# Moving the reciprocal row sums of a two-layer attention kernel by DMA through DRAM, instead of by widening, TensorE transposes and a ScalarE copy

## The chip, the cores and the metric

The kernel runs on one core of one Trainium2 chip. The metric is the device time in microseconds (us) of one execution. Some operations are named by engine: PE is TensorE, DVE is VectorE, ACT is ScalarE, POOL is GpSimd, SP is the engine whose queue issues the DMAs.

## The reference

Eight sequences of 256 tokens and width 256 pass through a gated routing layer (L0) and then through a transformer block. The block is self-attention (16 heads of 64), cross-attention to a context of 120 tokens, and a gated feed-forward layer of inner width 1024, each with a layer norm before it and a residual after it. The part that the change touches is the softmax of both attentions:

```python
h = layernorm(x, ln1_g, ln1_b)
x = attention(h, h, a1_Wq, a1_Wk, a1_Wv, a1_Wo, a1_bo) + x
h = layernorm(x, ln2_g, ln2_b)
x = attention(h, context, a2_Wq, a2_Wk, a2_Wv, a2_Wo, a2_bo) + x
# attention: attn = softmax(q k^T * SCALE); out = (attn @ v) @ Wo + bo
```

All of it is float32. Products are made from two rounded parts of each operand (hi and lo, three matmuls for one product).

## The kernel before

After L0 (to about 215 us) come 128 attention steps, `STEPS = 2 * B * PAIRS`: for each of the two attentions, for each sequence b of 8, for each pair of heads i of 8. Step G has b = G // 8 (0 to 7 self, 8 to 15 cross) and i = G % 8. Then come 8 feed-forward blocks (from about 935 us). Each engine has its own instruction list, written out by hand in `step_self(G)`, `step_cross(G)` and `feed_forward(b)`, and the engines meet only at semaphores. So the order on each engine is fixed, and an instruction that waits holds up all that stands behind it.

What happens to one pair of heads G:

- PE `scores(G)`, one step ahead; DVE `row_max(G)`; ACT `softmax_pair(G)` writes the unnormalised p and its row sums `expsum`, tokens on the partitions.
- DVE `inverse_sums(G)` (line 1096) opens DVE's step G: the reciprocal `rsum`, 128 tokens x (2 token tiles x 2 heads).
- PE `transpose_p(G)` (L1523), ACT `round_pT` (L731) and DVE `pT_low` (L1103) bring p into transposed hi and lo parts.
- PE `weighted_values(G)` in step G + 1 makes the output o in the transposed layout, 64 dimensions of each head on the partitions and 256 tokens in the free direction, in columns 0 to 255 of PSUM bank 6.
- Row sums stand per token, and in o the tokens lie along the free direction. So POOL `widen_sums(G)` (L531) copies each reciprocal 64 times into `rsw`, PE transposes `rsw` with two 128x128 transposes into columns 256 to 511 of bank 6 (L1538, the first thing that `weighted_values` does), and ACT `copy_rT(G)` (L735) brings that into SBUF as `rT`. The result is the reciprocal, repeated over the 64 partitions of each head.
- DVE `normalise_o(G)` (L1111), the last thing in DVE's step G + 1, multiplies o by `rT`; POOL `split_o(G)` splits the product; PE `project_out` uses it.

`weighted_values(G)` waits for `normalise_o(G - 1)`, because both use bank 6. Once per sequence comes the hand-over: `residual`, layer norm (`prepare_*`), storing and loading of the tokens by SP. Where two phases meet (b = 0, 7, 8 and 15), ACT and DVE also split the next weights (`weights_hi` L290, `weights_lo` L300), which SP loads in units of two 256 KB DMAs into four slots (`load_weights`, waits on `w_ready`). SP's list before is one loop over the 24 sequence turns: load, store, now and then a context or weights.

Of the kernel before, what the change touches and what calls it, by code (L numbers as in the profile page):

```python
# [26 lines left out]
NT = S // 128  # L27
# [93 lines left out]
def build(nc, x, ctx_p, weights, params, rows, ident_in, x1_dram, x2_dram, x3_dram, out):  # L121
    es = ExitStack()
    with es:
        def sb(name, shape, dt=F32, where=es):
            return where.enter_context(nc.sbuf_tensor(name, shape, dt))
# [78 lines left out]
        with ExitStack() as l1:  # L204
# [7 lines left out]
            with ExitStack() as att:  # L212
# [10 lines left out]
                rsw = sb("rsum_wide", [128, 2, NT, 2 * DH], where=att)  # L223
                rT = sb("rsumT", [128, S], where=att)
# [37 lines left out]
            "rsum_wide", "pT", "pT_hi", "pT_lo", "o", "rT_copied", "o_norm", "o_hi", "o_lo", "wo", "up", "gelu", "glu",  # L262
            "f_hi", "f_lo", "down")}
        NI = B // L0B

# [101 lines left out]
        def _(sp):  # L367
# [63 lines left out]

            load(0)
            load_context(B)
            load(1)
            load(2)
            for b in range(3 * B):
                if b + 3 < 3 * B:
                    load(b + 3)
                store(b)
                if B < b + 3 < 2 * B:  # L440
                    load_context(b + 3)
                if b == 0:
                    load_weights(sp, 12, 16)
                if b == 6:
                    load_weights(sp, 16, 20)
                if b == 8:
                    load_weights(sp, 20, 24)
                if b == 14:
                    load_weights(sp, 24, 26)
# [4 lines left out]
        def _(pool):  # L454
# [74 lines left out]
            def widen_sums(G):  # L529
                pool.wait_ge(y["rsum"], G + 1)  # L530
                nc.gpsimd.tensor_tensor(rsw[:, G % 2, :, :].rearrange("p t (e d) -> p (t e) d", e=2),  # L531
                                        rs[:, G % 2, :].unsqueeze(2).broadcast_to([128, NT * 2, DH]),
                                        ones[:, :].rearrange("p (n d) -> p n d", d=DH), ALU.mult
                                        ).then_inc(y["rsum_wide"], 1)

# [7 lines left out]
            def step(G):  # L543
                b, i = divmod(G, PAIRS)
                widen_sums(G)
# [20 lines left out]
        def _(act):  # L566
# [166 lines left out]
            def copy_rT(G):  # L733
                act.wait_ge(y["o"], G + 1)
                nc.scalar.copy(rT[:, :], bank[6][:, S:2 * S]).then_inc(y["rT_copied"], 1)  # L735

# [18 lines left out]
            def step_self(G):  # L755
# [31 lines left out]
                if G >= 1:  # L787
                    copy_rT(G - 1)

            def step_cross(G):  # L790
# [26 lines left out]
                copy_rT(G - 1)  # L817

            def feed_forward(b):
                it = b - 2 * B  # L820
                for j in range(FF // 128):
# [7 lines left out]
                    if j == 1 and it == 0:  # L829
                        copy_rT(STEPS - 1)  # L830
                        weights_hi(act, 25)
# [972 lines left out]
```

## Time and profile before

| | us |
|---|---|
| median of 3 runs (lowest, highest) | 1088.32 (1087.79, 1089.55) |
| profiled execution, its own time | 1088.15 |
| its span, first to last instruction | 1086.4 |
| PE busy in the span | 997.5 (92%) |
| DVE busy | 710.9 (65%) |
| ACT busy | 626.5 (58%) |
| POOL busy | 357.2 (33%) |
| mean granted TensorE clock | 0.969 of full speed |

The matmuls are pipelined: the duration of one is longer than the distance to the next, so a busy PE is not a measure of its rate. The distance from start to start is. What an operation is worth is read from the stretch in which it stands and from what ends last there.

### The profile page before, as it was taken

The numbers are of one execution on the slowest core, as the hardware profiler recorded it, in microseconds if no ns is written. First come the engines' busy times: TensorE is split into PE (matmuls) and PEld (weight loads), VectorE is DVE, ScalarE is ACT, GpSimd is POOL, SyncE is SP. The second block draws the span as 40 slices with busy tenths as digits, with TensorE's granted clock in tenths as the row PEclk, the third lists the DMA queues.
The fourth block names the chain that finished last, engine by engine and source line by source line (L and its number), as shares of the span: only waits on it lengthen the run. The fifth ranks groups of instructions, "written<-read, shape, count | busy, mean of one in ns | idle before, by whom it ended". The sixth has DMA issues, their size and how long they took to land.

```text
span 1086.4 us, 21327 instructions
## 1 busy us (share of the span) xinstructions
PE 997.5 (92%) x7872; PEld 937.3 (86%) x7872; DVE 710.9 (65%) x1598; ACT 626.5 (58%) x1945; POOL 357.2 (33%) x474
## 2 busy tenths in 40 slices
PE   5688874599999999999999999999999998899998
PEld 4577753489999999899999899999999997899998
DVE  4466744596766676667667775666677667566664
ACT  3466452386656575657566765666666666533333
POOL 1101324033334333333333244454554454401010
PEclk9999887699999999999999998999999999999999
DMA  6221000100200000000000300300000001010100
GB/s 205 68 68 39 20 20 20 44 11 2 98 2 21 1 21 1 21 1 21 2 21 3 101 25 1 103 25 2 25 26 18 8 21 46 17 38 21 40 30 21
DMA packets 28121, 34.62 MB, mean 32 GB/s; under 512 B 2164, under 2 KB 21364, under 8 KB 28020
## 3 DMA queue, kind: packets, MB, share of 16 engines
q1 hardware_dynamic: 28020, 33.26, 9.9%
q8 instruction: 65, 1.06, 0.4%
q14 instruction: 36, 0.29, 0.1%
HBM read 24.86 MB, written 8.39 MB: 31 GB/s over the span
## 4 chain that ended last, share of the span: by engine, by line
PE 79%; DVE 10%; ACT 6%; issue 2%; POOL 1%; DMA 1%; SPq 1%; DVEq 0%; POOLq 0%
PE bank L1306 17%; PE bank L1307 16%; PE bank L1308 16%; PE bank L1523 8%; PE bank L1506 5%; PE bank L1564 3%; PE bank L1565 3%; PE bank L1566 3%; PE bank L1538 3%; ACT p L721 1%; PE bank L1480 1%; PE bank L1414 1%; DVE bn L887 1%; PE bank L1415 1%; PE bank L1416 1%
## 5 line engine op out<-in xcount | busy, mean ns | idle before, releaser
L721 ACT ACTIVATE p<-bank,negmax 128x256 f32<-128x256 f32 (+1 forms) x512 | 208.2, 428 | 18.0 <-DVE negmax L1088 15.1
L538 POOL TENSOR_TENSOR oT_hi<-oT,ones 128x256 fp32r<-128x256 f32 x128 | 94.0, 735 | 378.0 <-DVE oT L1111 378.0
L731 ACT CAST pT_hi<-bank 128x512 fp32r<-128x512 f32 (+1 forms) x256 | 110.7, 485 | 166.1 <-PE bank L1523 165.3
L1306 PE MATMUL bank<-hT_hi,w_hi 128*128 128x256 f32 x640 | 190.6, 298 | 5.9 <-DVE hT_lo L1072 2.5
L1308 PE MATMUL bank<-hT_hi,w_lo 128*128 128x256 f32 x640 | 181.5, 284 | 0.0
L1307 PE MATMUL bank<-hT_lo,w_hi 128*128 128x256 f32 x640 | 181.3, 283 | 0.0
L1306 PEld LDWEIGHTS bank<-hT_hi,w_hi 128*128 128x128 f32 x640 | 122.6, 192 | 9.2 <-DVE hT_lo L1072 4.8
L1103 DVE TENSOR_TENSOR pT_lo<-bank,pT_hi 128x512 fp32r<-128x512 f32 (+1 forms) x256 | 129.7, 548 | 0.3
L1084 DVE TENSOR_REDUCE negmax<-bank 128x2 f32<-128x512 f32 x128 | 82.2, 684 | 66.8 <-PE bank L1506 66.8
L1307 PEld LDWEIGHTS bank<-hT_lo,w_hi 128*128 128x128 f32 x640 | 122.9, 192 | 0.0
L1308 PEld LDWEIGHTS bank<-hT_hi,w_lo 128*128 128x128 f32 x640 | 122.6, 192 | 0.0
L1306 PE MATMUL bank<-pT_hi,v_hi 128*128 128x256 f32 (+1 forms) x384 | 119.5, 311 | 0.0
L721 ACT ACTIVATION_READ_ACCUMULATOR p<-bank,negmax 128x1 f32 x512 | 110.2, 215 | 0.0
L1307 PE MATMUL bank<-pT_lo,v_hi 128*128 128x256 f32 (+1 forms) x384 | 109.1, 284 | 0.0
L1523 PE MATMUL bank<-ident,p 128*128 128x128 f32 (+1 forms) x768 | 109.1, 278 | 0.1
L1308 PE MATMUL bank<-pT_hi,v_lo 128*128 128x256 f32 (+1 forms) x384 | 109.0, 284 | 0.0
L540 POOL TENSOR_TENSOR oT_lo<-oT,oT_hi 128x256 fp32r<-128x256 f32 x128 | 95.1, 743 | 10.0
L1523 PEld LDWEIGHTS bank<-ident,p 128*128 128x128 f32 (+1 forms) x768 | 83.6, 140 | 9.0 <-ACT p L721 0.5
L531 POOL TENSOR_TENSOR rsum_wide<-rsum,ones 128x256 f32<-128x256 f32 x128 | 80.1, 626 | 17.6 <-DVE rsum L1096 17.6
L825 ACT ACTIVATE p<-bank,params_pp 128x256 f32<-128x256 f32 x64 | 30.4, 475 | 82.5 <-PE bank L1308 82.4
L1307 PEld LDWEIGHTS bank<-pT_lo,v_hi 128*128 128x128 f32 (+1 forms) x384 | 74.1, 193 | 0.0
L1308 PEld LDWEIGHTS bank<-pT_hi,v_lo 128*128 128x128 f32 (+1 forms) x384 | 74.0, 193 | 0.0
(200 smaller groups left out, 2787.2 us busy)
## 6 DMA issues: line engine op xcount, KB each, us to landing
w_stage<-in_weights SPq DMA_DIRECT2D x52, 256.0 KB, 4.8
x_in<-x_dram SPq DMA_DIRECT2D x24, 256.0 KB, 2.9
x_dram<-x_out SPq DMA_DIRECT2D x16, 256.0 KB, 3.2
l_x<-in_x SPq DMA_DIRECT2D x4, 512.0 KB, 5.6
x_dram<-l_out SPq DMA_DIRECT2D x4, 512.0 KB, 2.9
out_dram<-x_out SPq DMA_DIRECT2D x8, 256.0 KB, 3.1
l_ctx<-in_ctx SPq DMA_DIRECT2D x4, 240.0 KB, 5.3
ctx_in<-in_ctx SPq DMA_DIRECT2D x8, 120.0 KB, 3.2
```

Source lines behind the costliest of these rows:

```text
L531: nc.gpsimd.tensor_tensor(rsw[:, G % 2, :, :].rearrange("p t (e d) -> p (t e) d", e=2), rs[:, G % 2, :].unsqueeze(2).broadcast_to([128, NT ...
L538: nc.gpsimd.tensor_tensor(oh[:, G % PAIRS, :], of[:, :], ones[:, :], ALU.mult).then_inc(y["o_hi"], 1)
L540: nc.gpsimd.tensor_tensor(ol[:, G % PAIRS, :], of[:, :], oh[:, G % PAIRS, :].bitcast(F32), ALU.subtract).then_inc(y["o_lo"], 1)
L721: last = nc.scalar.activation(p[:, G % 2, e, t * cols:(t + 1) * cols], scores_at(G, e, t), ACT.Exp, bias=negmax[:, G % 2, t, e:e + 1], acc ...
L731: nc.scalar.copy(pTh[0:r, G % 2, e, 0:n], bank[4 + e][0:r, 0:n]).then_inc(y["pT_hi"], 1)
L1084: nc.vector.tensor_reduce(negmax[:, G % 2, :, e], score_bank(G, e)[:, :].rearrange("p (t n) -> p t n", t=NT), AX.X, ALU.max, negate=True). ...
L1103: nc.vector.tensor_tensor(pTl[0:r, G % 2, e, 0:n], bank[4 + e][0:r, 0:n], pTh[0:r, G % 2, e, 0:n].bitcast(F32), ALU.subtract).then_inc(y[" ...
L1306: nc.tensor.matmul(dst, lh, rh, start=(i == 0), stop=False)
L1307: nc.tensor.matmul(dst, lh, rl, start=False, stop=False)
L1308: last = nc.tensor.matmul(dst, ll, rh, start=False, stop=(i == n - 1))
L1506: last = nc.tensor.matmul(score_bank(G, e)[:, t * S:(t + 1) * S], lhs[pr, g, 0, tt], rhs[pr, g, 1, :], start=(n == 0), stop=(n == 2))
L1523: last = nc.tensor.transpose(bank[4 + e][0:n, j * S + t * 128:j * S + (t + 1) * 128], p[:, G % 2, e, t * cols + j * 128:t * cols + j * 128 ...
```

## The change

- `widen_sums`, the two transposes of `weighted_values` and `copy_rT` are gone, with the buffer `rsw` and the wait of PE for it.
- `inverse_sums` writes `rsum` ordered head, token tile, and waits that the DMA of two steps before has read the buffer.
- SP gets `spread_sums(G)`: it waits for `rsum`, writes 2 KB to DRAM (256 runs of two numbers, 8 bytes each, since the row in DRAM is ordered token, token tile), waits until that has landed, and issues two DMAs that read a row of 1 KB and write it to 64 partitions each. `rT` is now double.
- `normalise_o` waits for both DMAs and for PE's o, and reads `rT` with a stride of two numbers.
- SP's list is written anew around `spread_sums`: one call for each step, with stores at i = 3, loads at i = 4, contexts at i = 5, and the units of weights one by one, each behind a `spread_sums`.

```diff
-                rsw = sb("rsum_wide", [128, 2, NT, 2 * DH], where=att)
-                rT = sb("rsumT", [128, S], where=att)
+                rT = sb("rsumT", [128, 2, S], where=att)
...
+        sums_dram = nc.dram_tensor("rsums_dram", (2, 2, S), F32, kind="Internal").ap()
...
+            def spread_sums(G):
+                sp.wait_ge(y["rsum"], G + 1)
+                if G >= 2:
+                    sp.wait_ge(y["rT"], 32 * (G - 1))
+                sp.dma_start(sums_dram[G % 2, :, :].rearrange("e (q t) -> q e t", t=NT),
+                             rs[:, G % 2, :].rearrange("q (e t) -> q e t", e=2)).then_inc(y["rsum_row"], 16)
+                sp.wait_ge(y["rsum_row"], 16 * (G + 1))
+                if G >= 2:
+                    sp.wait_ge(y["o_norm"], G - 1)
+                for e in range(2):
+                    sp.dma_start(rT[e * DH:(e + 1) * DH, G % 2, :], sums_dram[G % 2, e:e + 1, :].partition_broadcast(DH)
+                                 ).then_inc(y["rT"], 16)
...
-            load(2)
-            for b in range(3 * B):
-                if b + 3 < 3 * B:
-                    load(b + 3)
-                store(b)
-                if B < b + 3 < 2 * B:
-                    load_context(b + 3)
-                if b == 0:
-                    load_weights(sp, 12, 16)
-                if b == 6:
-                    load_weights(sp, 16, 20)
-                if b == 8:
-                    load_weights(sp, 20, 24)
-                if b == 14:
-                    load_weights(sp, 24, 26)
+            for G in range(STEPS):
+                b, i = divmod(G, PAIRS)
+                spread_sums(G)
+                if i == 3 and b >= 1:
+                    store(b - 1)
+                if i == 4:
+                    load(b + 2)
+                if i == 5 and B < b + 2 < 2 * B:
+                    load_context(b + 2)
+                if b == 1 and i < 4:
+                    load_weights(sp, 12 + i, 13 + i)
+                if b == B - 1 and i >= 2 and i < 6:
+                    load_weights(sp, 14 + i, 15 + i)
+                if b == B + 1 and i < 4:
+                    load_weights(sp, 20 + i, 21 + i)
+                if b == 2 * B - 1 and i in (6, 7):
+                    load_weights(sp, 18 + i, 19 + i)
+            store(2 * B - 1)
+            for b in range(2 * B, 3 * B):
+                if b + 2 < 3 * B:
+                    load(b + 2)
+                store(b)
...
             def inverse_sums(G):
                 dve.wait_ge(y["exp"], 2 * G + 2)
-                nc.vector.reciprocal(rs[:, G % 2, :], expsum[:, G % 2, :, :].rearrange("p t e -> p (t e)")
+                if G >= 2:
+                    dve.wait_ge(y["rsum_row"], 16 * (G - 1))
+                nc.vector.reciprocal(rs[:, G % 2, :].rearrange("p (e t) -> p e t", e=2), expsum[:, G % 2, :, :].rearrange("p t e -> p e t")
...
             def normalise_o(G):
-                dve.wait_ge(y["rT_copied"], G + 1)
+                dve.wait_ge(y["rT"], 32 * (G + 1))
+                dve.wait_ge(y["o"], G + 1)
...
-                nc.vector.tensor_tensor(of[:, :], bank[6][:, 0:S], rT[:, :], ALU.mult).then_inc(y["o_norm"], 1)
+                nc.vector.tensor_tensor(of[:, :].rearrange("p (t q) -> p t q", t=NT),
+                                        bank[6][:, 0:S].rearrange("p (t q) -> p t q", t=NT),
+                                        rT[:, G % 2, :].rearrange("p (q t) -> p t q", t=NT), ALU.mult).then_inc(y["o_norm"], 1)
...
-                pe.wait_ge(y["rsum_wide"], G + 1)
...
-                for t in range(NT):
-                    nc.tensor.transpose(bank[6][:, S + t * 128:S + (t + 1) * 128], rsw[:, G % 2, t, :], ident[:, :])
```

## Rows read from the trace of the kernel before

**Rows 1.** The page: busy time of the engines, and the lines of the chain.

```profile
PE 997.5 (92%) x7872; PEld 937.3 (86%) x7872; DVE 710.9 (65%) x1598; ACT 626.5 (58%) x1945; POOL 357.2 (33%) x474
PE bank L1306 17%; PE bank L1307 16%; PE bank L1308 16%; PE bank L1523 8%; PE bank L1506 5%; PE bank L1564 3%; PE bank L1565 3%; PE bank L1566 3%; PE bank L1538 3%; ACT p L721 1%; PE bank L1480 1%; PE bank L1414 1%; DVE bn L887 1%; PE bank L1415 1%; PE bank L1416 1%
```

**Rows 2.** Windows, self stage and cross stage: length, busy (count), clock, DMA.

```profile
215.00:580.00 365.00, 364.27 (x3128) 337.11 (x3127) 254.09 (x528) 236.85 (x722) 128.71 (x184) 1.00 0.05 17
...
660.00:905.00 245.00, 239.69 (x1994) 233.82 (x1994) 165.56 (x416) 160.51 (x647) 118.85 (x169) 1.00 0.08 25
```

**Rows 3.** Waits of PE, 220 to 940 us: total, times, longest.

```profile
PE bank L1538 <- DVE oT L1111: 14.3, 11, 2.3
```

**Rows 4.** Timeline of PE in a self step: start, duration, instruction.

```profile
405.86 0.28 PE L1308 MATMUL bank<-hT_hi,w_lo 128*128 128x256 f32 x1
405.99 0.38 PE L1538 MATMUL bank<-ident,rsum_wide 128*128 128x128 f32 x2
...
406.32 0.28 PE L1307 MATMUL bank<-pT_lo,v_hi 128*128 128x256 f32 x1
406.44 0.28 PE L1308 MATMUL bank<-pT_hi,v_lo 128*128 128x256 f32 x1
```

**Rows 5.** Timeline of PE, the same place in a cross step.

```profile
776.19 0.28 PE L1308 MATMUL bank<-hT_hi,w_lo 128*128 128x256 f32 x1
...
776.65 0.28 PE L1307 MATMUL bank<-pT_lo,v_hi 120*128 120x256 f32 x1
```

**Rows 6.** Groups of PE by form, and of ACT: busy, mean ns, idle before.

```profile
L1538 PE MATMUL bank<-ident,rsum_wide 128*128 128x128 f32 x256 | 49.5, 275 | 14.3 <-DVE oT L1111 14.3
...
L735 ACT COPY rsumT<-bank 128x256 f32<-128x256 f32 x128 | 49.4, 386 | 8.7 <-PE bank L1308 1.1
```

**Rows 7.** Timeline of DVE in a self sequence, reciprocal and normalisation of G = 30.

```profile
402.28 0.17 DVE L1096 RECIPROCAL rsum<-expsum 128x4 f32<-128x4 f32 x1
...
414.75 0.41 DVE L1111 TENSOR_TENSOR oT<-bank,rsumT 128x256 f32<-128x256 f32 x1
```

**Rows 8.** Timeline of DVE in a cross sequence, G = 91, and one sequence later.

```profile
760.10 0.17 DVE L1096 RECIPROCAL rsum<-expsum 128x4 f32<-128x4 f32 x1
...
767.56 0.42 DVE L1111 TENSOR_TENSOR oT<-bank,rsumT 128x256 f32<-128x256 f32 x1 [0.84 <-ACT rsumT L735]
...
797.85 0.17 DVE L1096 RECIPROCAL rsum<-expsum 128x4 f32<-128x4 f32 x1
```

**Rows 9.** Timeline of PE: the transposes that follow the normalisation of G = 91.

```profile
771.45 0.38 PE L1538 MATMUL bank<-ident,rsum_wide 128*128 128x128 f32 x2
```

**Rows 10.** DMA issues, KB, us to landing: page; 1060 to 1090 us; timeline of SP.

```profile
x_in<-x_dram SPq DMA_DIRECT2D x24, 256.0 KB, 2.9
x_dram<-x_out SPq DMA_DIRECT2D x16, 256.0 KB, 3.2
...
out_dram<-x_out SPq DMA_DIRECT2D x2, 256.0 KB, 2.1
...
l_rows_bc<-in_rows SPq DMA_DIRECT2D x3, 128.0 KB, 4.4
...
3.76 1.38 SPq L397 DMA_DIRECT2D l_rows_bc<-in_rows  x3
```

**Rows 11.** Timelines of DVE and PE in the last cross sequence.

```profile
920.49 1.22 DVE L300 TENSOR_TENSOR w_lo<-w_stage,w_hi 128x1024 fp32r<-128x1024 f32 x1 [1.89 <-ACT w_hi L290]
921.63 0.42 DVE L1111 TENSOR_TENSOR oT<-bank,rsumT 128x256 f32<-128x256 f32 x1
...
922.19 0.41 PE L1538 MATMUL bank<-ident,rsum_wide 128*128 128x128 f32 x2 [2.25 <-DVE oT L1111]
```

**Rows 12.** Timelines where the last weights are split: DVE, then PE.

```profile
926.70 0.17 DVE L1096 RECIPROCAL rsum<-expsum 128x4 f32<-128x4 f32 x1
...
937.64 0.38 PE L1538 MATMUL bank<-ident,rsum_wide 128*128 128x128 f32 x2
```

**Rows 13.** Window after a wait in the first cross sequence; the clock is third from last.

```profile
648.00:656.00 8.00, 8.00 (x41) 8.00 (x39) 2.75 (x7) 3.60 (x13) 3.31 (x5) 0.50 0.01 3
```

More of the change, by code:

```diff
@@ L261, in build @@
             "cT_hi", "cT_lo", "qk", "qk_hi", "qk_lo", "v", "v_hi", "v_lo", "scores", "negmax", "exp", "rsum",
-            "rsum_wide", "pT", "pT_hi", "pT_lo", "o", "rT_copied", "o_norm", "o_hi", "o_lo", "wo", "up", "gelu", "glu",
+            "rsum_row", "rT", "pT", "pT_hi", "pT_lo", "o", "o_norm", "o_hi", "o_lo", "wo", "up", "gelu", "glu",
             "f_hi", "f_lo", "down")}
         NI = B // L0B
+        sums_dram = nc.dram_tensor("rsums_dram", (2, 2, S), F32, kind="Internal").ap()
         def wcols(name, kt, lo_col, n):
@@ L527, in add_bias @@
                                         ALU.add).then_inc(y["xb"], 1)
[L529 to L534, printed above, removed]
             def split_o(G):
@@ L544, in step @@
                 b, i = divmod(G, PAIRS)
-                widen_sums(G)
                 if i == 0:
@@ L731, in round_pT @@
                     nc.scalar.copy(pTh[0:r, G % 2, e, 0:n], bank[4 + e][0:r, 0:n]).then_inc(y["pT_hi"], 1)
-            def copy_rT(G):
-                act.wait_ge(y["o"], G + 1)
-                nc.scalar.copy(rT[:, :], bank[6][:, S:2 * S]).then_inc(y["rT_copied"], 1)
             def round_self(b, g):
@@ L786, in step_self @@
                     weights_hi(act, 10 + i)
-                if G >= 1:
-                    copy_rT(G - 1)
             def step_cross(G):
@@ L816, in step_cross @@
                     weights_hi(act, 17 + i)
-                copy_rT(G - 1)
             def feed_forward(b):
@@ L829, in feed_forward @@
                     if j == 1 and it == 0:
-                        copy_rT(STEPS - 1)
                         weights_hi(act, 25)
```

## Prediction

> **What bounds the kernel now.** I read the busy times first: PE is busy for 92% of the span, the next engine, DVE, for 65% [rows 1]. Matmuls overlap here, so that alone proves little. The chain of what ended last says the same by another way: its long shares are all PE lines, and the transposes at L1538, which the change removes, hold 3% of it [rows 1]. The windows by stage then show where. In 365 us of the self stage PE is idle for 0.7 us; in 245 us of the cross stage for 5.3 us; the granted clock is 1.00, the 2.4 GHz level, in both [rows 2]. The waits of PE name one cause almost alone: the first instruction of `weighted_values` waits 11 times, 14.3 us in all, for `normalise_o` of DVE [rows 3]. So in nearly every one of the 128 steps PE is what ends last. Work taken off PE comes off the time, while work taken off ACT and POOL does not by itself.
>
> **What goes.** Two transposes in each step. Their group is busy for 49.5 us, 275 ns each [rows 6], but what counts is the distance they put between neighbours. From the last projection matmul to the second matmul of `weighted_values` it is 406.32 - 405.86 = 0.46 us; undisturbed neighbours stand 0.12 us apart, so two such distances would be 0.24, and the pair costs 0.22 us [rows 4]. The cross stage has 776.65 - 776.19 = 0.46 at the same place, so 0.22 again [rows 5]. Times 64 that is 14.1 us in each stage, 28.2 in all.
>
> The Trainium skill ("TensorE: Matmul & The Clock Gate", Part 4) gives about 275 ns for such a transpose in a kernel, and says that the 2.4 GHz level does not engage for transposes. The first agrees with the duration here, but as a cost for 256 of them it would make 70 us, and start to start the trace gives less than half. The second the trace contradicts: the clock is 1.00 through the self stage with these transposes in every step.
>
> From that 28.2 I take what PE can't use:
>
> - *Self.* PE has next to no wait to hide in. Where the phases meet, ACT and DVE are loaded with weights; I let two steps go, 0.4 us. Left: 13.7.
> - *Cross.* Once in each sequence PE waits for `normalise_o`, and the pair that stands just before is parallel to DVE's chain (scale and shift, the hi part, `hT_lo`, `v_lo`, `normalise_o`). That pair only lengthens the wait: 8 pairs. In the last cross sequence DVE waits for ACT's high part of the weights, makes the low part (1.22), then `normalise_o`, and PE waits 2.25 us behind that [rows 11]. This ring has no transpose of the sums and no copy in it, so 4 more pairs are lost. 12 x 0.22 = 2.6. At the 11 waits themselves the transposes stand behind the wait; part of what they cost is the change of PE from float32 transposes to split matmuls, which the transposes of p cause as well. I take 0.05 less for each, 0.6. Left: 14.1 - 2.6 - 0.6 = 10.9.
>
> ACT's copy (49.4 us in all [rows 6]) and POOL's widening leave engines that don't bound; I count nothing for them. The nearest gain is DVE's wait for the copy, 0.84 us in [rows 8]; PE's next use of that result comes only at 771.45, 3.5 us after its end at 767.98 [rows 8, 9].
>
> **What comes, if it is in time.** The new way from reciprocal to `rT`: SP wakes, 0.14 us as PE does behind DVE (921.63 + 0.42 = 922.05, PE starts at 922.19 [rows 11]); the write lands; SP wakes again; one issue of 0.46 (1.38 / 3), then the second broadcast lands [rows 10]. No transfer of 2 KB is in the trace. The nearest store, 256 KB with nothing beside it, lands in 2.1 us, the usual one in 3.2; for the 64 KB broadcast the nearest are a load of 256 KB, 2.9, and the crowded broadcasts at the start, 4.4 [rows 10]. I take 2.1 and 2.9, since the payload is small and the queue mostly empty (DMA share 0.05 and 0.08 [rows 2]): 0.14 + 2.1 + 0.14 + 0.46 + 2.9 = 5.7 us. Low end, 2.1 twice: 4.9. High end: 0.14 + 3.2 + 0.14 + 0.46 + 4.4 = 8.3.
>
> The time there is: in self, from 402.45 to 414.75, 12.3 us [rows 7]; in cross, at the shortest place I found, from 760.27 to 767.56, 7.3 us [rows 8]. Two shorter steps take 0.4 off each. 5.7 fits both. The high end would hold DVE up by 1.4 us at the short place, where the 3.5 us of slack cover it. If the cover were gone, DVE would stand before its next reciprocal and `row_max`, and ACT's exponentials and then PE behind them.
>
> *SP's own turn.* SP waits for its write, so a step occupies it for 0.14 + 2.1 + 0.14 + 2 x 0.46 = 3.3 us, 4.4 at the high end. A cross step lasts (797.85 - 760.10) / 8 = 4.72 us [rows 8]. The stores, loads and contexts that share its list add three issues in eight steps, 0.17 us a step. Enough room, not plenty. SP's moved waits are for things that are done when it comes to them: `residual` of step i = 2 before the store of i = 3, `add_bias` of i = 3 before the load of i = 4. Early weights now come one unit a step and at least a step before their use.
>
> *The one late move.* Unit 24 of the weights is issued behind `spread_sums(126)`: 926.70 + 0.17 + 3.3 = 930.2, and 0.46 + 2.9 more until both halves are there, 933.5. ACT's part takes about what DVE's does, 1.2, then DVE's 1.2 and `normalise_o` 0.4: 936.3. PE wants that result at 937.64 [rows 10 to 12]. Hidden by 1.3 us; at 4.4 for a landing it would cost 0.2. Unit 25 has the feed-forward products before it.
>
> *DVE.* `normalise_o` reads `rT` at a stride of 8 bytes and has one wait more; the reciprocal too. The trace has no such strided read at this size; between 0 and a doubling of 0.42. PSUM is the other operand either way, so I take 0.05 us, and it counts only at the 11 waits: 0.5.
>
> **Sum.** 13.7 + 10.9 - 0.5 = 24.1 us. The profiled execution took 1088.15 (span 1086.4 and 1.7 around it); 1088.15 - 24.1 = 1064.0. The median is 0.2 higher. I say 1064.
>
> **Rivals.**
>
> - *Cross doesn't follow.* PE gets shorter, and the chain DVE, ACT, PE, with its 5.3 us of PE waits, becomes the limit through the whole stage. Against it: PE waits in only one step of eight. Then only self gains: 1088.3 - 13.7, about 1074 us.
> - *More than the pairs.* The ACT copy leaves the way of `normalise_o`, and some of the 14.3 us of waits go with it. Also, after a wait at 645 us PE runs busy for 8 us at 0.50, the 1.2 GHz level [rows 13]; a shorter wait there could keep the clock and give back 4. Against it: the waits hang on other work. About 1058.
> - *SP becomes the bound.* The write of 256 runs of 8 bytes is slow to land. With W for its landing SP needs W + 0.28 + 0.92 + 0.17 a step. From W = 3.35 that exceeds a cross step of 4.72, and from 3.35 + 13.7 / 64 = 3.56 it has eaten the gain of self too: slower than before. With W = 4.4, twice the nearest row, cross loses 64 x 1.05 = 67 us: 1088 + 67 - 14 = 1141. For it: nothing in the trace bounds such a pattern from above. Against it: 2 KB is little, and a store of 256 KB needs as many rows of 1 KB as this has runs.
> - *The transposes were no cost.* PE hides them in gaps of its own. Then nothing changes, 1088. Against it: the neighbours' distances.
>
> The Trainium skill speaks for the third ("DMA: Bandwidth & Descriptors", Specifications and Rules for kernel authors): pieces under 512 B are read, modified and written, and a plain DMA with a rearranged pattern is 19 times slower than the hardware's own transposing one. By 19 on the 2.1 us of the nearest store SP would take 41 us a step, an estimate from that page's factor alone. No row of before shows such pieces, so the trace can't say whether it holds here.
>
> **How the numbers follow.** Forecast 0.60 (1061 to 1068); cross doesn't follow 0.13; more than the pairs 0.14; SP the bound 0.07; no cost 0.06. The range from 1057 to 1074 holds the first three. A measurement of this kernel tells about 0.2% from no change, 2.2 us. Faster 0.87, same 0.06, slower 0.07.
>
> **What would show it.** PE has 256 instructions fewer and about 28 us less, and its neighbours before and in `weighted_values` stand 0.12 apart. The self sequence gets shorter by 8 x 0.22 = 1.8 us, the cross sequence (37.75) by 1.4 to 1.8. `normalise_o` doesn't wait for DMA, SP's write lands in 2 to 3.2 us and `rT` 5 to 8 us after the reciprocal. PE's waits for `normalise_o` in cross stay or grow a little. Wrong it would be if the write lands after 3.35 us or later, if waits for a DMA stand before `normalise_o` on DVE, or if ring waits turn up in other steps of a sequence.

## The result and the profile after

The changed kernel takes 1158.5 us (median of 4 runs, 1153.1 to 1165.4); the kernel before, run on the same chips, 1088.1 (1086.1 to 1089.6). The ratio is 1.066, with an interval from 1.0604 to 1.0717. I had forecast 1064, in a range from 1057 to 1074. The profiled execution took 1160.5, its span is 1158.7 against 1086.4: 72.3 us more. One execution of one version below (16 byte runs, broadcasts by POOL) took 1237.6 us at a granted clock of 0.741 and is left out of its times.

The page after, as [rows 1] and [rows 10] of before: busy times, DMA packets, the lines of the chain, then two of the DMA issues (KB each, us to landing).

```profile
PE 1015.9 (88%) x7616; PEld 943.2 (81%) x7616; DVE 705.0 (61%) x1598; ACT 587.4 (51%) x1817; POOL 281.0 (24%) x346
...
DMA packets 83418, 51.66 MB, mean 45 GB/s; under 512 B 41076, under 2 KB 76660, under 8 KB 83316
...
DMA rsums_dram<-rsum 32%; PE bank L1316 8%; PE bank L1317 8%; PE bank L1318 8%; SPq L443 7%; PE bank L1533 4%; PE bank L1516 3%; DMA rsumT<-rsums_dram 3%; SPq L277 1%; DVE bn L892 1%; PE bank L1424 1%; PE bank L1571 1%; PE bank L1572 1%; PE bank L1573 1%; PE bank L1425 1%
...
rsumT<-rsums_dram SPq DMA_DIRECT2D x256, 64.0 KB, 3.0
...
rsums_dram<-rsum SPq DMA_DIRECT2D x128, 2.0 KB, 4.0
```

The 256 transposes are gone from PE's count, yet the chain is no longer PE's. A third of it is the landing of the 2 KB write, and another 7% is SP's issue of the broadcasts. A write of 2 KB lands later (4.0 us) than a broadcast that moves 64 KB (3.0).

Windows, self stage and then the six cross sequences b = 9 to 14 (columns as in [rows 2]):

```profile
215.00:580.00 365.00, 359.98 (x3055) 331.43 (x3052) 257.42 (x534) 221.53 (x678) 96.35 (x127) 1.00 0.20 37
666.80:957.20 290.40, 248.99 (x1772) 234.69 (x1771) 150.31 (x385) 137.60 (x554) 82.13 (x108) 0.90 0.22 43
```

In cross PE was idle for 5.3 us of 245; now it is for 41.4 of 290.4, and the granted clock fell from 1.00 to 0.90. At two levels, 1.00 and 0.50, a mean of 0.90 over 290.4 us means 58 us at the lower one, 1.2 GHz. So PE loses time in two ways there: it waits, and after some of the waits it works at the lower level.

Waits over the whole run: of DVE, of PE (the same wait as in [rows 3]), and of SP's queue.

```profile
DVE oT L1119 <- DMA rsumT<-rsums_dram: 123.9, 52, 6.0
...
PE bank L1316 <- DVE oT L1119: 50.6, 34, 3.4
```

```profile
SPq L443 <- DMA rsums_dram<-rsum: 457.2, 128, 5.8
```

I had written that it would be wrong if DVE waited for a DMA ahead of `normalise_o`. It does, in 52 of 128 steps. SP waits before the broadcasts in all 128 steps, 3.6 us each.

The distance from a reciprocal to the same one eight steps later shows where the 72.3 us are. I read it from the starts of `inverse_sums`. The eight self sequences together are 2.7 us shorter: four are 1.73 shorter and one 1.45, but b = 0, 1 and 7, two of which have weights in SP's list, are 1.2, 3.0 and 1.5 longer. The cross stage is 68.7 longer: its inner sequences take 45.1 to 54.4 us, 48.4 in the mean, instead of 37.75. From the last reciprocal to the end it is 6.4 longer.

SP and DVE in a cross sequence, timelines (start, duration, instruction):

```profile
792.80 0.41 SPq L437 DMA_DIRECT2D rsums_dram<-rsum  x1
798.19 1.09 SPq L443 DMA_DIRECT2D rsumT<-rsums_dram  x2
799.38 0.53 SPq L420 DMA_DIRECT2D x_in<-x_dram  x1
800.00 0.42 SPq L437 DMA_DIRECT2D rsums_dram<-rsum  x1
804.35 1.09 SPq L443 DMA_DIRECT2D rsumT<-rsums_dram  x2
805.50 1.22 SPq L425 DMA_DIRECT2D ctx_in<-in_ctx  x1
806.82 0.37 SPq L437 DMA_DIRECT2D rsums_dram<-rsum  x1
...
797.19 0.42 DVE L1119 TENSOR_TENSOR oT<-bank,rsumT 128x256 f32<-128x256 f32 x1 [5.99 <-DMA rsumT<-rsums_dram]
797.53 0.17 DVE L1103 RECIPROCAL rsum<-expsum 128x4 f32<-128x4 f32 x1
```

SP has no gap: each item of its list begins 0.1 us behind the one before, or when a write has landed (5.39 us after its issue, then 4.35). Its turns are 7.20 and 6.82 us long, where a cross step of before is 4.72. The reciprocal of 797.53 is ready at 797.70, and SP takes it up at 800.00.

What a write spends its time on, in an undisturbed self step: SP's timeline, then the DMA engines' busy tenths over 403 to 410 us in 40 slices of 0.175 us.

```profile
403.89 0.37 SPq L437 DMA_DIRECT2D rsums_dram<-rsum  x1
407.72 1.08 SPq L443 DMA_DIRECT2D rsumT<-rsums_dram  x2
```

```profile
DMA  4366530000610000000000000000000000222232
```

The write's packets move in slices 10 and 11, 404.75 to 405.1. After them the engines stand still for 2.6 us, and only then SP goes on. So most of these 3.8 us are neither issue nor transfer, but the time until the landing is reported. The Trainium skill ("DMA: Bandwidth & Descriptors", Anatomy of one DMA) says of a DMA issued from GpSimd that of about 2 us fixed cost most is the confirmation by the target memory, and that this can be surprisingly long for DRAM; this row, of a DMA issued from SP, agrees in kind and has more than its figure.

### The profile page after: what moved, and what is told of

Its sections match the earlier page's. It is cut to its first block, busy times and chain, and to the rows that moved or that the text cites. A ratio compares the mean times of both kernels' runs of the same rounds, so it can differ in the third digit from the quotient of the medians.

```text
span 1158.7 us, 21194 instructions
## 1 busy us (share of the span) xinstructions
PE 1015.9 (88%) x7616; PEld 943.2 (81%) x7616; DVE 705.0 (61%) x1598; ACT 587.4 (51%) x1817; POOL 281.0 (24%) x346
## 2 busy tenths in 40 slices
DMA packets 83418, 51.66 MB, mean 45 GB/s; under 512 B 41076, under 2 KB 76660, under 8 KB 83316
## 3 DMA queue, kind: packets, MB, share of 16 engines
q8 instruction: 62, 1.02, 0.5%
## 4 chain that ended last, share of the span: by engine, by line
PE 38%; DMA 36%; SPq 10%; DVE 7%; ACT 4%; issue 2%; POOL 1%; DVEq 0%; POOLq 0%
DMA rsums_dram<-rsum 32%; PE bank L1316 8%; PE bank L1317 8%; PE bank L1318 8%; SPq L443 7%; PE bank L1533 4%; PE bank L1516 3%; DMA rsumT<-rsums_dram 3%; SPq L277 1%; DVE bn L892 1%; PE bank L1424 1%; PE bank L1571 1%; PE bank L1572 1%; PE bank L1573 1%; PE bank L1425 1%
## 5 line engine op out<-in xcount | busy, mean ns | idle before, releaser
L1316 PE MATMUL bank<-hT_hi,w_hi 128*128 128x256 f32 x640 | 193.7, 303 | 13.8 <-DVE qkT_lo L1144 5.4
L1317 PE MATMUL bank<-hT_lo,w_hi 128*128 128x256 f32 x640 | 184.1, 288 | 0.0
L1316 PE MATMUL bank<-pT_hi,v_hi 128*128 128x256 f32 (+1 forms) x384 | 115.0, 300 | 51.6 <-DVE oT L1119 50.6
L1316 PEld LDWEIGHTS bank<-hT_hi,w_hi 128*128 128x128 f32 x640 | 125.6, 196 | 18.3 <-issue 13.3
L1119 DVE TENSOR_TENSOR oT<-bank,rsumT 128x256 f32<-128x256 f32 x128 | 53.8, 420 | 124.3 <-DMA rsumT<-rsums_dram 123.9
L1317 PEld LDWEIGHTS bank<-hT_lo,w_hi 128*128 128x128 f32 x640 | 125.8, 197 | 0.0
L1318 PEld LDWEIGHTS bank<-hT_hi,w_lo 128*128 128x128 f32 x640 | 125.6, 196 | 0.0
L1316 PEld LDWEIGHTS bank<-pT_hi,v_hi 128*128 128x128 f32 (+1 forms) x384 | 75.2, 196 | 61.5 <-DVE oT L1119 60.6
L1533 PE MATMUL bank<-ident,p 128*128 128x128 f32 (+1 forms) x768 | 112.4, 284 | 0.6 <-DVE pT_lo L1110 0.3
L1533 PEld LDWEIGHTS bank<-ident,p 128*128 128x128 f32 (+1 forms) x768 | 86.3, 143 | 9.6 <-ACT p L734 1.0
```

The lines of the kernel that those rows point to most:

```text
L1119: nc.vector.tensor_tensor(of[:, :].rearrange("p (t q) -> p t q", t=NT), bank[6][:, 0:S].rearrange("p (t q) -> p t q", t=NT), rT[:, G % 2, ...
L1316: nc.tensor.matmul(dst, lh, rh, start=(i == 0), stop=False)
L1317: nc.tensor.matmul(dst, lh, rl, start=False, stop=False)
L1318: last = nc.tensor.matmul(dst, ll, rh, start=False, stop=(i == n - 1))
L1533: last = nc.tensor.transpose(bank[4 + e][0:n, j * S + t * 128:j * S + (t + 1) * 128], p[:, G % 2, e, t * cols + j * 128:t * cols + j * 128 ...
```

## The experiments

Distances per sequence below are from reciprocal to reciprocal, cross sequences are those with b = 9 to 14 (before: 37.75).

**The wait for the write taken out.** The broadcasts read a constant row of 1 KB instead of the sums, so `rT` holds no reciprocals; write and traffic stay. SP no longer has to wait for the landing.

```diff
-                sp.wait_ge(y["rsum_row"], 16 * (G + 1))
...
-                    sp.dma_start(rT[e * DH:(e + 1) * DH, G % 2, :], sums_dram[G % 2, e:e + 1, :].partition_broadcast(DH)
...
+                    sp.dma_start(rT[e * DH:(e + 1) * DH, G % 2, :], rows[1:2, :].partition_broadcast(DH)
...
```

> The changed kernel with one dependence cut: the two broadcasts read a constant row of DRAM (a gain vector) instead of the row sums, so SP need not wait until its write has landed. All three DMAs of a step, their sizes and their issue times stay. The output is normalised by wrong numbers. Theory A (SP's turn: wait for the write plus issues, about 6 us a step against 4.72): the wait is gone, SP is busy for 1.6 us a step, so the cross sequences return to 36 to 36.5 us and the kernel to 1062 to 1070. Theory C (the 38,900 added packets themselves slow the DMAs and the engines): stays at 1140 or more. Theory B (only the length of the way to rT counts) also expects about 1065, as the way gets shorter by the write; this run does not part A from B.

1064.8 us (1063.1 to 1066.1), ratio 0.9778 (0.9757 to 0.9798). Its windows, self and cross:

```profile
215.00:580.00 365.00, 364.28 (x3122) 336.23 (x3121) 263.43 (x545) 225.76 (x690) 98.01 (x129) 1.00 0.17 39
660.00:880.00 220.00, 215.50 (x1760) 207.97 (x1760) 152.53 (x391) 135.78 (x558) 83.72 (x110) 1.00 0.24 55
```

Self sequences are 49.99, cross 36.27. Everything that the change adds is there except this one wait, and the time is the one that I had forecast. The 38,912 more packets under 512 B (41,076 against 2,164 before) cost nothing that shows; the wait costs 94 us. But without it both SP's turn and the way to `rT` are shorter, so this run doesn't say which of the two bound; the next ones do in part.

**The broadcasts issued by POOL.** SP only writes; POOL waits for the landing at the head of its step. The way of one step stays as long, but SP doesn't stand in it.

```diff
+            def broadcast_sums(G):
+                pool.wait_ge(y[f"row{G % 2}"], 16 * (G // 2 + 1))
+                if G >= 2:
+                    pool.wait_ge(y["o_norm"], G - 1)
+                for e in range(2):
+                    nc.gpsimd.dma_start(rT[e * DH:(e + 1) * DH, G % 2, :], sums_dram[G % 2, e:e + 1, :].partition_broadcast(DH)
+                                        ).then_inc(y[f"rT{G % 2}"], 16)
```

> The changed kernel with the two broadcasts issued by POOL, which waits for the write in SP's place; nothing else moves (two semaphores are split by parity). The way from reciprocal to rT keeps its length, about 8 us alone; SP is busy for about 0.5 us a step. Theory A (SP's turn is the ring that sets the cross steps): cross sequences fall from 45 to 54 us to 37 to 39, kernel 1070 to 1085. Theory B (the length of the way, against 7.3 us of room, sets it): little changes, cross stays over 44 us, kernel over 1140. If POOL's own issues are slow (over 2 us for each) POOL becomes the ring and cross stays slow with the write issued on time; the trace would show the write at 0.1 us behind the reciprocal and late broadcasts.

1102.4 us (1099.8 to 1106.5), ratio 1.0116 (1.0086 to 1.0147).

```profile
DVE oT L1122 <- DMA rsumT<-rsums_dram: 50.3, 29, 5.1
```

Windows, b = 12 and b = 13:

```profile
783.80:826.90 43.10, 40.50 (x308) 39.27 (x307) 25.09 (x64) 22.57 (x92) 22.35 (x34) 0.92 0.24 41
...
826.90:863.10 36.20, 35.50 (x292) 34.28 (x291) 24.84 (x65) 22.44 (x92) 22.56 (x35) 1.00 0.23 49
```

SP's lateness (reciprocal to issue of the write, median over cross) falls from 2.7 us to 0.03, and DVE's waits from 123.9 to 50.3. The mean cross sequence is 41.9 against 48.4, so about 6.5 of the 10.6 us that a sequence had lost went with SP's turn. From reciprocal to `rT` it is still 9.0 us in the median, more than the 7.3 that the short places have, and 4 us stay. They aren't simply DVE's waits. Between the reciprocals that bound b = 13 DVE waited three times for `rT`, 3.3 us in all, and the sequence still took 36.2 us, as with the wait cut: the clock stayed at 1.00. The other five, each with 6.8 to 13.7 us at the lower level and longer waits of PE, took 41.1 to 44.0; how the 4 us divide between waits and clock isn't measured. Both forecasts missed: 1102.4 lies between the 1070 to 1085 of the one theory and the 1140 of the other.

**The new order of SP's list, alone, on the kernel before.** SP waits for `rsum` in each step, but writes and broadcasts nothing.

```diff
...
-            for b in range(3 * B):
...
+            for G in range(STEPS):
+                b, i = divmod(G, PAIRS)
+                sp.wait_ge(y["rsum"], G + 1)
+                if i == 3 and b >= 1:
+                    store(b - 1)
...
```

> The kernel before, with its widening, transposes and copy, but with SP's new list of loads, stores and weights; in place of the three DMAs SP only waits for the reciprocal of each step. Theory D (the moved weights and loads cost time by themselves): over 1091. Otherwise 1086 to 1090, and the late weights are only late behind the waits for the write.

1088.9 us, ratio 1.0004 (0.9986 to 1.0022). So the new places of the stores, loads and weights cost nothing by themselves.

**The write measured by itself.** At the end of the kernel before, with nothing else running, SP issues single DMAs and waits for each.

```diff
+            for k in range(3):
+                for out_ap, in_ap in (
+                    (pr["pairs"].rearrange("e (q t) -> q e t", t=2), stage[:, 0, 0, 0:4].rearrange("q (e t) -> q e t", e=2)),
+                    (pr["quads"], stage[:, 0, 0, 0:4]),
...
+                    sp.dma_start(out_ap, in_ap).then_inc(probed, 16)
+                    probes += 1
+                    sp.wait_ge(probed, 16 * probes)
```

> The kernel before, with 27 single DMAs issued one after another, each waited for, behind its last store, when nothing else runs (its time is longer by them and says nothing). Stores to DRAM from 128 partitions: two runs of 8 B for each partition, side by side in DRAM as in the change (2 KB); one run of 16 B each, side by side; one of 16 B each, 512 B apart; two of 8 B each, 512 B apart; one run of 64 B, 512 B, 1 KB each. Then one small copy inside SBUF and one 64 KB broadcast from DRAM. Theory C1 (small pieces that share a stretch of DRAM are merged one after another): 8 B side by side 3.0 to 3.4 us, 16 B side by side 2.6, both 512 B apart 2.1 or less, 1 KB rows 2.1. Theory C2 (any piece under 512 B costs): all of them up to 64 B stand at about 3, apart or not. Theory C3 (the pattern does not matter, the time in the kernel is the queue's): all at about 2.1. The copy inside SBUF is expected at 1.6 to 2.1.

SP's timeline, second round. Each starts when the one before has landed, so a difference of starts is a landing:

```profile
1100.69 0.38 SPq L469 DMA_DIRECT2D probe_pairs<-w_stage  x1
1103.96 0.33 SPq L469 DMA_DIRECT2D probe_quads<-w_stage  x1
1105.37 0.32 SPq L469 DMA_DIRECT2D probe_quads_apart<-w_stage  x1
1106.77 0.56 SPq L469 DMA_DIRECT2D probe_pairs_apart<-w_stage  x1
1108.67 0.32 SPq L469 DMA_DIRECT2D probe_rows64b<-w_stage  x1
1110.07 0.32 SPq L469 DMA_DIRECT2D probe_rows512b<-w_stage  x1
1111.60 0.32 SPq L469 DMA_DIRECT2D probe_rows1k<-w_stage  x1
1113.29 0.48 SPq L469 DMA_DIRECT2D half_b<-rstd  x1
```

The change's pattern (`pairs`, 256 runs of 8 bytes side by side) takes 3.3 us; the same 2 KB as 128 runs of 16 bytes (`quads`) takes 1.4, beside each other or 512 bytes apart; the 8 byte runs 512 bytes apart take 1.9; 128 rows of 1 KB take 1.7. The theory that had 8 byte runs slow side by side was right on those, and wrong on the 16 byte ones, for which it had 2.6. The Trainium skill ("DMA: Bandwidth & Descriptors", Specifications) has pieces under 512 B read, modified and written. No step shows at 512 B here: 64 bytes land in 1.4 us, 512 bytes in 1.5.

A second set asks whether it is the size, the number or the place of the runs.

```diff
+                    (pr["one8"], stage[:, 0, 0, 0:2]),
+                    (pr["one8_of16"][:, 0:2], stage[:, 0, 0, 0:2]),
...
+                    (pr["one4"], stage[:, 0, 0, 0:1]),
+                    (pr["two16"].rearrange("e (q t) -> q e t", t=4), stage[:, 0, 0, 0:8].rearrange("q (e t) -> q e t", e=2)),
```

> Single stores to DRAM behind the last store of the kernel before, each waited for, three times each. All from 128 partitions where nothing else is said: the form of the change again (256 pieces of 8 B, 3.3 us); the same from 64 partitions; 128 pieces of 8 B side by side; 128 of 8 B every 16 B; 256 of 8 B every 16, 32 and 64 B; 128 of 4 B side by side; 256 of 16 B and 256 of 64 B side by side. Theory C1 (pieces under 16 B that share a small stretch of DRAM are written one behind another): side by side 8 B and 4 B slow even with 128 pieces (over 2 us), every 16 B slower than every 64 B, 256 of 16 B no slower than 2.0. Theory C4 (the number of pieces and the jump between a partition's two runs): 128 pieces of any form 1.4, 256 of any form 2.0 to 3.3, whatever their size and distance.

```profile
1113.97 0.36 SPq L471 DMA_DIRECT2D probe_pairs<-w_stage  x1
1117.25 0.59 SPq L471 DMA_DIRECT2D probe_pairs_half<-w_stage  x1
1120.89 0.34 SPq L471 DMA_DIRECT2D probe_one<-w_stage  x1
1124.11 0.33 SPq L471 DMA_DIRECT2D probe_one_of<-w_stage  x1
1125.52 4.33 SPq L471 DMA_DIRECT2D probe_pairs_of<-w_stage  x3
1131.05 0.33 SPq L471 DMA_DIRECT2D probe_one<-w_stage  x1
1138.26 2.87 SPq L471 DMA_DIRECT2D probe_two<-w_stage  x2
```

Side by side, 128 runs of 4 bytes take 7.2 us (the last `probe_one`), 128 of 8 bytes 3.2 (the first), 128 of 8 bytes in two rows 3.6; 256 of 16 or of 64 bytes take 1.5 in the median of three rounds (one of 16 bytes took 2.5). Set apart, 256 runs of 8 bytes, each at the head of its own 16, 32 or 64 bytes, take 1.5, 1.6 and 1.5 in the median, 128 of them 1.4 in this round but 2.5 and 2.4 in the others, and 512 bytes apart it was 1.9. So the number of runs is not what counts: 16 bytes and more land fast in either place, and runs of 4 and 8 bytes land slowly above all where they lie against each other.

The packets of these writes, told by their size in the traces, show where the time goes. In the rounds shown the last packet ends 1.13 us after the issue for the change's pattern, 1.01 for `quads` and 1.02 for the runs of 4 bytes, and the landings come at 3.26, 1.39 and 7.19. So nearly the whole difference lies behind the last packet: 2.1, 0.4 and 6.2 us until the landing is reported. Why the report comes so late for short adjacent runs, these runs don't show.

**The write as 128 runs of 16 bytes.** The row in DRAM keeps the order token, head, tile. The broadcasts read 2,040 bytes for each head from its own offset, twice the bytes, and `normalise_o` reads at a stride of four numbers.

```diff
-                sp.dma_start(sums_dram[G % 2, :, :].rearrange("e (q t) -> q e t", t=NT),
-                             rs[:, G % 2, :].rearrange("q (e t) -> q e t", e=2)).then_inc(y["rsum_row"], 16)
+                sp.dma_start(sums_dram[G % 2, :].rearrange("(q x) -> q x", x=4), rs[:, G % 2, :]).then_inc(y["rsum_row"], 16)
...
+                    sp.dma_start(rT[e * DH:(e + 1) * DH, G % 2, 0:2 * S - 2],
+                                 sums_dram[G % 2:G % 2 + 1, 2 * e:2 * e + 2 * S - 2].partition_broadcast(DH)
...
```

> The changed kernel, all of the reference computed, with another form of the write: each of the 128 partitions stores its four numbers as one run of 16 B, side by side (128 pieces in place of 256 of 8 B). Each head's broadcast reads 510 numbers from its own offset, and the normalisation reads them at a stride of four. The broadcasts carry twice the bytes. If the form of the write is what makes it slow, it lands 1.9 us sooner, as the single DMAs showed (1.4 against 3.3), in the kernel at about 2.1; SP's turn is 3.5 us against 4.7, the way to rT 5.5 to 6.3 us: cross sequences 36.3 to 37, kernel 1063 to 1070. If the time of the write is the queue's or the waits' whatever its form, it lands at over 3.3 still and the kernel stays over 1100.

1081.2 us (1077.4 to 1084.2), ratio 0.9923 (0.9903 to 0.9943). With another pattern of the write, and nothing else but the reading that goes with it, the change is 0.8% faster than before instead of 6.6% slower. The forecast of 1063 to 1070 fell short, though:

```profile
L1119 DVE TENSOR_TENSOR oT<-bank,rsumT 128x256 f32<-128x256 f32 x128 | 77.1, 602 | 20.3 <-DMA rsumT<-rsums_dram 19.8
...
rsums_dram<-rsum SPq DMA_DIRECT2D x128, 2.0 KB, 2.3
```

The write lands in 1.6 us in self (median), but in 2.7 in cross. By its packets (medians, self and cross) 0.8 and 1.2 us go from issue to the first, 0.2 and 0.6 from the first to the last, 0.5 and 0.7 from the last to the landing. In cross the broadcasts of the step before land 2.0 us after the write is issued, in self 0.5 before it, so in cross both are under way at once. DVE still waits 19.8 us for `rT`, and the stride of four costs 0.18 us a step (602 against 420 ns for the stride of two).

The same on the POOL version:

> The same with the two broadcasts issued by POOL as well. With SP's turn already short nothing is left for it to give: within 0.3% of the run before it, 1062 to 1070. If SP's turn (loads, stores and weights behind it) still costs, 2 to 6 us less than with SP alone, in the sequences with weights.

1082.9 us (1075.7 to 1084.5), ratio 0.9938 (0.9916 to 0.996), no different from the one with SP, and above the forecast like it. With a short write SP's turn is no longer what binds.

**The reciprocal earlier.** In cross DVE takes it right behind `pT_low`, ahead of the rest of its step.

```diff
+                if G == STEPS // 2:
+                    inverse_sums(G)
-                inverse_sums(G)
...
                 pT_low(G)
+                if more or i < PAIRS - 1:
+                    inverse_sums(G + 1)
```

On the changed kernel:

> The changed kernel (1158.5 us) with one thing moved: in the second eight sequences VectorE takes the reciprocal of the next step right behind the two remainders of p (pT_lo), ahead of the other work of its step, some 1.6 us earlier than before. Theory A (SP's turn is the bound there: write 4.1, its issue, two broadcasts and their issue make up the 5.97 us of a step): a ring that is full doesn't care when the reciprocal is there; 1150 to 1160. Theory B (the way from the reciprocal to rT is merely longer than the room it has): 1.6 us less at each of the steps at which VectorE waits for rT, 52 of them; about 1158 - 52*1.6 = 1075 to 1100.

1145.8 us (1141.3 to 1148.8), ratio 1.0544 (1.0502 to 1.0585). Timelines of SP and of DVE:

```profile
799.26 1.09 SPq L443 DMA_DIRECT2D rsumT<-rsums_dram  x2
...
801.09 0.37 SPq L437 DMA_DIRECT2D rsums_dram<-rsum  x1
...
796.46 0.17 DVE L1103 RECIPROCAL rsum<-expsum 128x4 f32<-128x4 f32 x1
```

The reciprocal is ready at 796.63 and waits 4.5 us for SP. Over cross the median of that wait rises from 2.7 to 5.4 us: nearly all of what DVE gives earlier becomes waiting for SP. That is the mark of a full ring. The time still fell by 12.7 us (ratio 1.054 after 1.066), further than the 1150 to 1160 of the ring theory and far from the 1075 to 1100 of the other, so the ring explains the bulk, and the remainder isn't explained.

On the version with 16 byte runs:

> The same early reciprocal on the version with the write as 128 runs of 16 B (1081.2 us, write 2.7 in the second half). VectorE waited for rT 19.8 us in 14 steps of 660 to 905, 1.4 us each: an earlier reciprocal by 1.6 covers nearly all of it. 1081 - 19.8*64/51 = 1056 at the very least; since its normalise_o with a stride of four elements costs 605 against 420 ns, 0.19 a step, part of that stays: forecast 1064 to 1072. If 1078 or more, the wait wasn't what cost the rest, and VectorE's own work or the weights at the end is.

1077.4 us (1072.1 to 1077.8), ratio 0.9915 (0.9883 to 0.9947), its profiled execution the fastest of them (span 1070.3). The waits of DVE:

```profile
DVE oT L1119 <- DMA rsumT<-rsums_dram: 2.9, 2, 1.8
```

Windows, b = 9, 10 and 12:

```profile
652.90:692.70 39.80, 38.68 (x293) 37.51 (x292) 26.85 (x64) 22.73 (x93) 13.77 (x18) 0.91 0.41 118
692.70:729.30 36.60, 35.48 (x293) 34.32 (x292) 26.80 (x64) 22.57 (x92) 13.77 (x18) 1.00 0.35 78
...
765.90:805.70 39.80, 38.68 (x292) 37.51 (x292) 26.87 (x64) 22.72 (x92) 13.77 (x18) 0.91 0.34 73
```

The wait for `rT` is gone, and the undisturbed cross sequences take 36.6 us, 0.3 from those without the wait. So there the way was too long for its room. But b = 9 and 12 take 39.8, and the gain in time is no more than the scatter between runs; the forecast of 1064 to 1072 was missed again. What holds b = 9 and 12 is the clock: PE is idle for 1.1 us in each of the three windows, but in those two 6.8 us ran at the 1.2 GHz level, and they are 3.2 us longer. Before the clock fell PE had waited 1.05 us for `normalise_o`; it waited as long in the other sequences, where the clock stayed. What decides between them isn't shown.

On the POOL version:

> The same early reciprocal on the version whose broadcasts POOL issues (1102.4 us), where SP only writes and the ring is two queues long. VectorE waited there for rT at 20 of 47 traced steps of the second half, 5.1 us each, 39.7 us within 660 to 905. If what was left is latency alone, 20*1.6 = 32 us times 64/47 at most comes off: 1070 to 1085. If it was queueing behind the stores and loads, little does: 1095 to 1102.

1113.8 us, ratio 1.0262 (1.0224 to 1.03), slower than without it. This one was ill made: there SP's write of G waits for `normalise_o(G - 2)`, and that now stands on DVE behind the reciprocal of G. The write can't go earlier (its issue comes 2.3 us after the reciprocal; without the move it was 0.03), while DVE pays 30.7 us of waits for the exponentials. It tells nothing of the latency.

**The new way in self, the old one in cross.**

```diff
...
+                if G >= STEPS // 2:
+                    return
...
+                if G >= STEPS // 2:
+                    pe.wait_ge(y["rsum_wide"], G + 1 - STEPS // 2)
+                    for t in range(NT):
+                        nc.tensor.transpose(bank[6][:, S + t * 128:S + (t + 1) * 128], rsw[:, G % 2, t, :], ident[:, :])
```

> The way of the change in the self stage alone; in the cross stage widening, transposes and copy as before. SP keeps the new list. The self stage of the changed kernel was 2.8 us shorter than before in all (1.73 us in each undisturbed sequence, given back in the three with weights or with short first steps), and cross returns to 37.75 us a sequence. Kernel 1084 to 1088. If the self stage also costs something later, over 1088.

1077.4 us (1075.7 to 1078.4), ratio 0.9901 (0.9886 to 0.9915). The inner cross sequences are 37.73 as before, self is 49.99 but for b = 7 (56.25), and b = 0 and 1 don't lose anything here, though SP's list is the same in self. Of the 12.5 us between the profiled executions 9.7 come from self and 2.9 from the first cross sequence (41.36 against 44.29), where the clock was low for 6.9 us instead of 10.2. The forecast of 1084 to 1088 was too high by both. With the write as 16 byte runs in its self part:

> The mixed version (DMA way in the first eight sequences, TensorE transposes in the second, 1077.4 us) with the write of the first half as 128 runs of 16 B. Its first half already ran at 49.99 us a sequence but for the eighth (56.25 against 53.3 with no wait for the write). The shorter write gives back up to 3 us there and the 0.19 us longer normalise_o takes nothing where VectorE is idle: 1074 to 1077.5.

1078.2 us (1075.5 to 1079.8), ratio 0.9925 (0.9898 to 0.9952), the same within the scatter and just above its forecast. These two and the last 16 byte version are the best that I have, all about 1% faster than the kernel before.

## Why the prediction was wrong

- *The gain on PE: right.* In the step of [rows 4] the last projection matmul and the second of `weighted_values` now stand 0.24 us apart:

```profile
407.06 0.28 PE L1318 MATMUL bank<-hT_hi,w_lo 128*128 128x256 f32 x1
...
407.18 0.28 PE L1316 MATMUL bank<-pT_hi,v_hi 128*128 128x256 f32 x1
...
407.30 0.28 PE L1317 MATMUL bank<-pT_lo,v_hi 128*128 128x256 f32 x1
```

An undisturbed self sequence is 1.73 us shorter, 8 x 0.217. Where the wait is cut, cross sequences are 1.48 shorter, within my 1.4 to 1.8, and the kernel takes 1064.8. The sum of 24.1 us fits a way that is in time, with some luck: the profiled execution of that run is 23.5 us shorter, 12.6 in self instead of my 13.7, 12.3 in cross instead of 10.9, and 1.1 longer in the tail, for which I had no term. Of the 12.3, 3.5 are the first cross sequence alone, where the clock was low for 6.8 us instead of 10.2, as the rival "more than the pairs" had it. "Cross doesn't follow" and "no cost" are refuted by that run.
- *The landing of the write: the step that failed.* "I take 2.1 and 2.9, since the payload is small and the queue mostly empty." The nearest row was a store of 256 KB in rows of 1 KB, and I let it stand for 256 runs of 8 bytes. Alone this write takes 2.7 to 4.2 us, in the kernel 3.7 in self and 4.1 in cross (medians). Even my high end, 3.2, was under both medians. The trace had no such row, so the upper bound that I drew was none, and I gave the rival that needed it 0.07.
- *SP's own turn: too short by the same term.* I had 3.3 us, 4.4 at most, against a step of 4.72. Issue and landing are 4.3 in the mean in cross, the pair of broadcasts 1.08 instead of 0.92, and the stores, loads and contexts come on top: a turn is over the 4.72, and the cross step became 5.97. The rival "SP becomes the bound", with its point of decision at 3.35 us, is what happened. Its formula with 4.34 gives 5.71 a step, 63 us in cross and 1138 in all. The profiled execution took 1160.5: 11 of the other 22 us are the gain that self didn't keep, 6.4 the tail, 5.3 cross. (The 4.4 that the rival calls twice the nearest row isn't: twice 2.1 is 4.2, which gives 1129.)
- *The clock: a term that I didn't have.* I let lost waits cost their own length. In b = 9 to 14 PE was idle for 41.4 us, 36 more than before, yet these six sequences are 64 us longer, though the transposes are gone; 58 us of them ran at the 1.2 GHz level. By the 3.2 us that 6.8 such us cost in the last 16 byte version, 58 cost about 27: an estimate. No run here holds the clock and keeps the waits, so the split isn't measured.
- *The way to `rT`: too short, and late in self too.* I had 5.7 us; it is 7.8 in self and 11.1 in cross (medians), where 2.7 of it is SP's lateness. In self 12.3 us of room cover it in most sequences. b = 7, with weights in SP's list, takes 55.8 to 56.3 in the three versions where SP waits for the slow write, and 53.3 where the wait is cut or POOL issues the broadcasts. b = 0 and 1 lost 1.2 and 3.0 us in the changed kernel and nothing in the mixed one with the same list, so the weights alone don't explain b = 1.
- *The late move of unit 24: not hidden.* Timelines of SP and of ACT at the end of cross:

```profile
994.70 1.48 SPq L437 DMA_DIRECT2D rsums_dram<-rsum  x1
998.81 1.08 SPq L443 DMA_DIRECT2D rsumT<-rsums_dram  x2
999.95 1.05 SPq L277 DMA_DIRECT2D w_stage<-in_weights  x2
...
1003.78 1.05 ACT L290 CAST w_hi<-w_stage 128x1024 fp32r<-128x1024 f32 x1 [7.56 <-DMA w_stage<-in_weights]
```

The reciprocal of step 126 starts at 991.27. I had the unit 3.5 us behind it; it is issued 8.7 us behind: SP is 3.3 late with the write, and the write takes 4.1. ACT waits 7.6 us for the weights, and the tail of the kernel is 6.4 longer. How much of that is this unit and how much the next, which stands behind one more turn, wasn't tried.
- *DVE's strided read: no cost.* In the mixed version it takes 415 ns at a stride of two numbers and 417 in the plain form; 420 in the changed kernel. The 0.5 us that I took off for it wasn't due.
- *The Trainium skill ("DMA: Bandwidth & Descriptors", Rules for kernel authors) spoke for the right rival, by the wrong amount.* A factor of 19, or 41 us a step, was far off; 4.1 instead of 2.1 was enough.
- *The clock with transposes: read too far.* The prediction takes the 1.00 of self as a contradiction. But the ten transposes of a self step take about 1.1 of its 6.5 us (0.11 each), and matmuls fill the rest; what a stretch of transposes alone would be granted no run here shows.

Open: why adjacent short runs are reported so late; why the 16 byte write, 1.4 us alone, takes 2.7 in cross (it is later in all its parts while the broadcasts of the step before are still on their way, but no run takes those away); and which of PE's waits are followed by a fall of the clock.

## What to carry to other kernels

A small DMA isn't priced by its bytes. If it stands in a ring (issue, wait for landing, issue again, all on one queue), its landing time times the steps is compared with the step, and a pattern that no row of the trace shows is measured by itself before one builds on it. When one queue is the ring, an earlier producer gives little (12.7 us here); a shorter landing (77 us) or a second queue (56 us) gives much. A wait of PE can cost more than its length, so the granted clock of each stage is read before the rest of a loss is put down to something else. And a step that feeds another engine should be replaced stage by stage: here the same change pays where a step lasts 6.2 us and takes the gain away where it lasts 4.7.

## What the runs showed of the hardware

- Writes of 2 KB or less from 128 partitions to DRAM, alone: 1.4 us as 16 byte runs, 3.3 as adjacent 8 byte runs, 7.2 as adjacent 4 byte runs, though the last is a quarter of the bytes. Runs of 8 bytes set apart: 1.4 to 2.5.
- The transfer itself is short in the slow pattern too: in the kernel 0.5 us from the first packet to the last in self and 0.6 in cross (medians). From the last packet to the reported landing it is 2.0 and 2.1 us with adjacent 8 byte runs, 0.5 and 0.7 with 16 byte runs.
- 6.8 us at the 1.2 GHz level made two cross sequences of the last 16 byte version 3.2 us longer (39.8 against 36.6), with the same idle time of PE.
- `normalise_o`, 128x256, reads `rT` at a stride of two numbers in 415 to 420 ns, as without a stride (417), and at a stride of four in 602.
- The granted clock in the first cross sequence, after PE's wait of about 2 us there, decides some 2 us. The window of 8 us behind that wait, first of the mixed version, then of the same with 16 byte runs (the clock is third from last):

```profile
640.00:648.00 8.00, 8.00 (x45) 7.70 (x45) 4.75 (x11) 4.19 (x14) 2.36 (x4) 0.69 0.06 17
```

```profile
640.00:648.00 8.00, 8.00 (x39) 8.00 (x39) 3.21 (x7) 4.02 (x14) 2.87 (x5) 0.50 0.16 47
```

  The second has the whole window at 0.50, the 1.2 GHz level, as [rows 13], the first only part of it, and its sequence b = 8 is 2.25 us shorter (41.36 against 43.61). The work in both is the same.
